# A decoder layer on one core: self-attention with a longer lag between its engines, and another order where cross-attention begins

## The reference, cut to what matters

```
x = layernorm(x + self_attention(x))            # 32 heads of 16, ALiBi bias, causal mask, biases b_qkv and b_out
x = layernorm(x + cross_attention(x, ctx))      # 32 query heads of 128, 8 key/value heads, rotary positions, mask
x = layernorm(x + ffn(x))                       # relu^2 FFN of 1024, plus routed latent path, own layernorm inside
```

## Time and profile before

| | us |
|---|---|
| median of 3 runs | 930.53 (929.92 to 932.32) |
| profiled execution | 930.1 |
| its span, first to last instruction | 928.3 |
| busy in the span: TensorE | 875.9 (94%) |
| VectorE | 679.0 (73%) |
| ScalarE | 487.6 (53%) |
| GpSimd | 497.0 (54%) |
| mean granted TensorE clock | 0.986 of full |
| moved by DMA | 96.65 MB |

### The profile page before, as it was taken

How to read it: one execution, slowest core, us unless ns; L and a number is a source line. 1 busy time by engine, 2 the same in 40 slices (tenths; PEclk the granted TensorE clock), 3 DMA queues, 4 the chain that set the end, 5 groups by cost and what they waited for, 6 DMA issues and landing times.

```text
span 928.3 us, 15683 instructions
## 1 busy us (share of the span) xinstructions
PE 875.9 (94%) x4780; PEld 722.0 (78%) x4780; DVE 679.0 (73%) x2203; ACT 487.6 (53%) x1541; POOL 497.0 (54%) x422
## 2 busy tenths in 40 slices
PE   7998889999997989999999999999999998999996
PEld 6786667777775778888888888888888887787884
DVE  5557678988887677777777777777777778556646
ACT  5327678787786255555555555555555556341320
POOL 4625832242227566666666666666666688564001
PEclk9999899999999989999999999999999999999998
DMA  8678987696566401131311312213113122000000
GB/s 279 246 200 228 243 140 159 160 178 142 126 183 224 162 34 35 35 126 35 128 43 35 125 35 73 88 35 126 35 35 126 41 73 93 18 29 24 24 12 34
DMA packets 68371, 96.65 MB, mean 104 GB/s; under 512 B 7232, under 2 KB 44352, under 8 KB 67264
## 3 DMA queue, kind: packets, MB, share of 16 engines
q1 hardware_dynamic: 68288, 95.65, 36.4%
HBM read 68.33 MB, written 27.26 MB: 103 GB/s over the span
## 4 chain that ended last, share of the span: by engine, by line
PE 64%; DVE 13%; issue 8%; ACT 7%; POOL 5%; DMA 1%; SPq 1%; POOLq 0%; ACTq 0%; DVEq 0%
PE banks L35 55%; PE banks L1107 4%; ACT B_prob L677 3%; DVE B_prob L838 3%; PE banks L1087 3%; PE banks L1108 2%; DVE B_t L902 1%; DVE B_t L903 1%; POOL x L1624 1%; DMA heads_k<-heads_k_d 1%; ACT B_v_out L655 1%; POOL C_t L1212 1%; DVE B_t L898 1%; ACT C_prob L1038 1%; POOL B_wv L171 1%
## 5 line engine op out<-in xcount | busy, mean ns | idle before, releaser
L35 PE MATMUL banks<-C_wo,C_o 128*128 128x512 f32 x768 | 191.2, 398 | 1.9 <-DVE C_o L1199 1.0
L35 PE MATMUL banks<-xT,C_w 128*128 128x512 f32 x768 | 185.6, 390 | 3.1 <-DVE xT L137 1.5
L35 PEld LDWEIGHTS banks<-xT,C_w 128*128 128x128 f32 x768 | 143.9, 188 | 33.9 <-issue 4.2
L35 PEld LDWEIGHTS banks<-C_wo,C_o 128*128 128x128 f32 x768 | 140.2, 189 | 30.4 <-issue 1.9
L1029 ACT ACTIVATE C_q<-C_t 128x512 fp32r<-128x512 f32 x64 | 40.5, 632 | 166.0 <-POOL C_t L1212 166.0
L677 ACT ACTIVATE B_prob<-B_prob,B_top 128x128 f32<-128x128 f32 x256 | 99.4, 392 | 33.4 <-DVE B_top L838 33.2
L1220 POOL TENSOR_TENSOR C_q<-C_t,C_q 128x512 fp32r<-128x512 f32 x64 | 82.9, 1295 | 47.5 <-ACT C_q L1029 47.5
L1038 ACT ACTIVATE C_prob<-C_prob,C_top 128x128 f32<-128x128 f32 x256 | 99.0, 391 | 1.2 <-DVE C_top L1171 1.2
L1212 POOL TENSOR_TENSOR C_t<-C_t,C_t 128x512 f32<-128x512 f32 x64 | 82.7, 1293 | 5.1 <-DVE C_t L1152 4.9
L171 POOL TENSOR_TENSOR C_w<-stage,C_w 128x512 fp32r<-128x512 f32 x32 | 41.8, 1308 | 53.7 <-ACT C_w L166 53.7
L171 POOL TENSOR_TENSOR C_wo<-stage,C_wo 128x512 fp32r<-128x512 f32 x32 | 41.1, 1287 | 54.2 <-ACT C_wo L166 54.2
(11 more groups left out here) (146 smaller groups left out, 1916.4 us busy)
## 6 DMA issues: line engine op xcount, KB each, us to landing
C_kv<-cross_kv_d SPq DMA_DIRECT2D x8, 2048.0 KB, 8.7
cross_kv_d<-B_k_out SPq DMA_DIRECT2D x16, 512.0 KB, 3.3
cross_kv_d<-B_v_out SPq DMA_DIRECT2D x16, 512.0 KB, 4.9
stage<-wq_dram SPq DMA_DIRECT2D x32, 256.0 KB, 2.6
stage<-wo_dram SPq DMA_DIRECT2D x32, 256.0 KB, 2.6
heads_q<-heads_q_d SPq DMA_DIRECT2D x96, 64.0 KB, 3.9
heads_k<-heads_k_d SPq DMA_DIRECT2D x96, 64.0 KB, 4.0
heads_q_d<-cT SPq DMA_DIRECT2D x8, 512.0 KB, 2.6
```

The lines of the kernel that those rows point to most:

```text
L35: mm = eng.matmul(out, stationary[i], moving[j], start=first and n == 0, stop=last and n == len(PASSES) - 1)
```

## The change

Five things are changed, all in order, lag or place; no arithmetic is added or left out.

1. Lags in B: `LT` 2 to 3, `LV` 4 to 6, the whole closing of a batch two steps later (`OT` 11 to 13 and so on); `value_lo` one step after `value_hi` instead of in the same step; `key_lo` and both stores one step later.
2. The output bias `bout` moves to memory of its own (126 KB; there a weight half of cross-attention is written at step 61, which now waits for the eighth addition). So the first oT tile no longer waits for all additions. Each batch's x row is loaded in its step 1 and gets the bias in its step 5.
3. SyncE loads the last four context pieces ahead of the first heads.
4. The `_end` parts are written in another order, with one more transpose, weighing and row addition in them, and query tiles spread between.
5. Cross steps 0 to 2 have orders of their own: `tensor_first` (transposes between the halves of a query tile), `vector_first`, and on ScalarE the exponentials of step 1 behind the pT copy in step 2, and tile 6's high half behind the o copy.

The diff, with little of its unchanged surroundings:

```diff
@@ -305,14 +305,13 @@
                 self.load_piece(eng, self.CONTEXT + (i - self.QK // 2) // 2)
+        for n in range(self.CONTEXT + C, len(self.pieces)):
+            self.load_piece(eng, n)
         heads.wait_stored(eng, self.QK // 2)
...
             ring.load(eng, n, sources[n])
-            if n == 0:
-                for j in range(self.CONTEXT + C, len(self.pieces)):
-                    self.load_piece(eng, j)
         heads.load(eng, 0, 1)
@@ -448,7 +447,7 @@
-    LT, LV = 2, 4
+    LT, LV = 3, 6
     NS = B * NG
@@ -458,7 +457,7 @@
-    OT, CLOSE, ROW, ROOT, NORMAL, TURN, TAKE = 11, (12, 13), 14, 15, 16, 17, 18
+    OT, CLOSE, ROW, ROOT, NORMAL, TURN, TAKE = 13, (14, 15), 16, 17, 18, 19, 20
     NEXT_LOAD = {57: range(5), 62: (5, 6), 64: (7,), 67: (8,)}
@@ -473,7 +472,7 @@
         self.k_out = [pool(f"k_out{i}", (96, 132)[i], [P, 4, 2, S], F32R) for i in range(2)]
-        self.bout = pool("bout", 100, [P, D])
+        self.bout = pool("bout", 126, [P, D])
         self.oT = [pool(f"oT{i}", 100 + 2 * i, [P, C, S], F32R) for i in range(2)]
@@ -533,22 +532,22 @@
                 self.heads.load(eng, later, i)
-            if n < B:
-                eng.dma_start(self.x1[:, n, :], self.dram["x_nat"][:, n, :]).then_inc(self.s_x[n], 16)
+            if n < self.NS and n % NG == 1:
+                eng.dma_start(self.x1[:, n // NG, :], self.dram["x_nat"][:, n // NG, :]).then_inc(self.s_x[n // NG], 16)
             if n == 1:
-                eng.wait_ge(self.before.s_acc, len(self.before.order))
+                eng.wait_ge(self.before.s_vlo, self.before.QK)
                 eng.dma_start(self.bout[:, :], self.dram["bout"]).then_inc(self.s_bout, 16)
...
                 loaded += 1
-            j = self.tile("k", n, 3)
+            j = self.tile("k", n, 4)
             if j is not None:
...
                    .then_inc(self.s_kout[j % 2], 16)
-            j = self.tile("v", n, 1)
+            j = self.tile("v", n, 2)
             if j is not None:
@@ -584,12 +583,18 @@
-        j = self.tile("k", n, 2)
+        j = self.tile("k", n, 3)
         if j is not None:
...
             self.rows.root(eng, b)
+        if n % NG == 5:
+            b = n // NG
+            if b == 0:
+                eng.wait_ge(self.s_bout, 16)
+            eng.wait_ge(self.s_x[b], 16)
+            eng.tensor_tensor(self.x1[:, b, :], self.x1[:, b, :], self.bout[:, :], ALU.add).then_inc(self.s_xadd, 1)
         j = self.tile("k", n, 1)
@@ -597,30 +602,29 @@
         self.gpsimd_pieces(eng, n)
-        b = n - 3
-        if 0 <= b < B:
-            if b == 0:
-                eng.wait_ge(self.s_bout, 16)
-            eng.wait_ge(self.s_x[b], 16)
-            eng.tensor_tensor(self.x1[:, b, :], self.x1[:, b, :], self.bout[:, :], ALU.add).then_inc(self.s_xadd, 1)
         if n in self.NEXT_SPLIT:
+            if self.NEXT_SPLIT[n] == 1:
+                eng.wait_ge(self.s_xadd, B)
             self.cross.piece_lo(eng, self.NEXT_SPLIT[n])
...
+        self.rows.root(eng, B - 2)
         self.key_lo(eng, len(self.FILL) // 2 - 1)
-        for i in range(3, 7):
+        for i in (3, 4):
             self.cross.piece_lo(eng, i)
         self.cross.tile_sum(eng, 0)
+        self.cross.piece_lo(eng, 5)
         self.cross.tile_lo(eng, 0)
-        self.cross.piece_lo(eng, 7)
         self.cross.tile_sum(eng, 1)
+        self.rows.root(eng, B - 1)
         self.cross.tile_lo(eng, 1)
-        self.rows.root(eng, B - 1)
+        self.cross.piece_lo(eng, 6)
         for r in (2, 3):
...
             self.cross.tile_lo(eng, r)
+        self.cross.piece_lo(eng, 7)
@@ -644,8 +648,6 @@
         wait(eng, self.s_y, b)
-        if b == 0:
-            eng.wait_ge(self.s_xadd, B)
         eng.activation(self.oT[0][:, :, :], self.ov[b % 2].rearrange("p (c s) -> p c s", c=C), ACT.Copy).then_inc(self.s_ohi, 1)
@@ -689,16 +691,19 @@
-        self.copy_turned(eng, self.NS - 2)
+        self.copy_turned(eng, self.NS - 3)
         self.key_hi(eng, len(self.FILL) // 2 - 1)
         self.value_hi(eng, len(self.FILL) // 2 - 1)
+        self.copy_turned(eng, self.NS - 2)
+        self.copy_turned(eng, self.NS - 1)
         eng.wait_ge(self.s_klo, len(self.FILL) // 2)
-        for i in range(3, 7):
+        for i in (3, 4):
             self.cross.piece_hi(eng, i)
-        self.copy_turned(eng, self.NS - 1)
         self.rows.hi(eng, B - 2)
+        self.output_hi(eng, B - 1)
+        for i in (5, 6):
+            self.cross.piece_hi(eng, i)
         self.cross.tile_hi(eng, 0)
-        self.output_hi(eng, B - 1)
         self.cross.piece_hi(eng, 7)
@@ -811,19 +816,21 @@
-        self.weigh(eng, (self.NS - self.LV) // 2)
+        self.transpose(eng, self.NS - 3)
+        self.weigh(eng, self.NS // 2 - 3)
         self.transpose(eng, self.NS - 2)
-        self.cross.project(eng, 0)
-        self.cross.project(eng, 1, (0, 1))
+        self.cross.project(eng, 0, (0, 1))
         self.transpose(eng, self.NS - 1)
+        self.weigh(eng, self.NS // 2 - 2)
+        self.cross.project(eng, 0, (2, 3))
         self.turn(eng, B - 2)
-        self.cross.project(eng, 1, (2, 3))
         self.weigh(eng, self.NS // 2 - 1)
-        self.cross.project(eng, 2, (0, 1))
+        self.cross.project(eng, 1)
         self.close(eng, B - 1, range(C))
-        self.cross.project(eng, 2, (2, 3))
-        self.cross.project(eng, 3)
+        self.cross.project(eng, 2)
+        self.cross.project(eng, 3, (0, 1))
         self.turn(eng, B - 1)
+        self.cross.project(eng, 3, (2, 3))
@@ -901,7 +908,7 @@
             eng.tensor_tensor(by_batch(t2[64:128, :]), by_batch(bank[0:64, :]), sin[64:128], ALU.mult).then_inc(self.s_sin, 1)
-        j = self.tile("v", n, 0)
+        j = self.tile("v", n, 1)
         if j is not None:
@@ -912,12 +919,13 @@
         self.norm(eng, self.NS - 1)
+        self.add_row(eng, B - 2)
+        self.value_lo(eng, len(self.FILL) // 2 - 1)
         self.rows.normalise(eng, B - 2)
-        self.value_lo(eng, len(self.FILL) // 2 - 1)
         eng.wait_ge(self.s_klo, len(self.FILL) // 2)
         self.cross.rotate(eng, 0)
+        self.output_lo(eng, B - 1)
         self.rows.lo(eng, B - 2)
-        self.output_lo(eng, B - 1)
         self.cross.rotate(eng, 1)
@@ -1045,13 +1053,23 @@
             eng.activation(self.pT[0][:, :], self.tp[n % 2], ACT.Copy).then_inc(self.s_phi, 1)
-        if n + self.PRE < self.TILES:
+        if n == 2:
+            self.exponentials(eng, 1)
+            self.next_piece_hi(eng, 1)
+        elif n + self.PRE < self.TILES:
             self.tile_hi(eng, n + self.PRE)
...
             eng.activation(self.o[0][:, :], self.ov, ACT.Copy).then_inc(self.s_ohi, 1)
-        self.exponentials(eng, n)
+        if n == 2:
+            self.tile_hi(eng, n + self.PRE)
+        if n != 1:
+            self.exponentials(eng, n)
+            self.next_piece_hi(eng, n)
+    def next_piece_hi(self, eng, n):
         i = self.split(n)
@@ -1135,10 +1153,19 @@
+        if n + self.PRE + 1 < self.TILES:
+            self.project(eng, n + self.PRE + 1)
+    def tensor_first(self, eng, n):
         if n == 0:
             self.project(eng, self.PRE)
-        if n + self.PRE + 1 < self.TILES:
-            self.project(eng, n + self.PRE + 1)
+        self.project(eng, n + self.PRE + 1, range(2))
+        self.transpose(eng, n)
+        self.project(eng, n + self.PRE + 1, range(2, C))
+        self.scores(eng, n)
+        self.values(eng, n)
@@ -1174,29 +1201,51 @@
+    def inverse(self, eng, m):
+        if 0 <= m < self.NS:
+            eng.wait_ge(self.s_exp, m + 1)
+            wait(eng, self.s_norm, m - 1)
+            eng.reciprocal(self.rden[:, m % 2, :], self.total[:, m % 2, :]).then_inc(self.s_rden, 1)
+    def turned_lo(self, eng, m):
+        if 0 <= m < self.NS:
+            eng.wait_ge(self.s_phi, m + 1)
+            eng.tensor_tensor(self.pT[1][:, :], self.tp[m % 2], self.pT[0][:, :].bitcast(F32),
+                              ALU.subtract).then_inc(self.s_plo, 1)
+    def output_lo(self, eng, m):
+        if 0 <= m < self.NS:
+            eng.wait_ge(self.s_ohi, m + 1)
+            eng.tensor_tensor(self.o[1][:, :], self.ov, self.o[0][:, :].bitcast(F32), ALU.subtract).then_inc(self.s_olo, 1)
+    def vector_first(self, eng, n):
+        if n < 2:
+            self.rotate(eng, n + self.PRE)
+        self.turned_lo(eng, n - 2)
+        self.inverse(eng, n - 1)
+        self.minima(eng, n)
+        self.output_lo(eng, n - 2)
+        if n == 2:
+            self.rotate(eng, n + self.PRE)
     def vector(self, eng, n):
-        if n == 1:
+        self.inverse(eng, n - 1)
+        if n + self.PRE < self.TILES:
             self.rotate(eng, n + self.PRE)
-        if self.live(n, 1):
-            eng.wait_ge(self.s_exp, n)
-            wait(eng, self.s_norm, n - 2)
-            eng.reciprocal(self.rden[:, (n - 1) % 2, :], self.total[:, (n - 1) % 2, :]).then_inc(self.s_rden, 1)
-        if n != 1 and n + self.PRE < self.TILES:
```

(21 more changed lines are left out.)

## The result

The changed kernel takes 921.39 us (median of 4 runs, 919.03 to 922.9) where the kernel before took 930.22 beside it: a ratio of 0.990, 95% interval 0.9869 to 0.9932. It is faster, by 8.8 us and not by the 17.3 forecast. The profiled execution took 922.72 us, its span is 920.9.

What follows compares the result with a forecast made beforehand. It took the loop as bound by VectorE's round with a 2.1 us wait, TensorE close behind and full from 337.5 us. Terms 9 + 6.8 + 1.5 = 17.3 off 930.1 gave 912.8, plus 0.4 for the median: 913, range 903 to 926.

Steps and rivals of the forecast that it cites:

- the likeliest case: Whole run: all three gains arrive, 17.3 us in sum, giving 913 us, own range 907 to 919; chance 0.52.
- Part 1: Start of the self-attention loop: spread x loads and bias additions save 9 us, bounds 3 and 11.
- scores of step 8 at 98.6: Start, TensorE: with fewer x loads ahead of batch 1's heads, these scores come at 98.6 instead of 100.97 us.
- rival (b): Start stays DMA-bound, head loads being small and slow; it gains only 3 us, total 919; chance 0.12.
- Part 2: Self-attention loop: VectorE's 2.1 us and TensorE's 0.9 us waits go; batch 25.53 to 24.4, gain 6.8 us, bounds 0 and 10.4.
- A bare VectorE step takes 1.71 us: Loop: VectorE's step without passes, taken as 1.71 us in the eight-step table that closed the round at 24.15 us.
- rival (c): GpSimd's moved bias additions hold up VectorE's divisions, 0.6 to 1.3 us in seven batches; total 917 to 922; chance 0.11.
- Part 3: Last batch and first cross steps to TensorE's second value product: 1.5 us saved of 49.5, bounds -3 and +8.
- The queue in cross step 2: Rotation, sum, copy, exponentials, next rotation and pT half in a row put the second value product 46.2 us after the loop.
- (a): Loop keeps its period, the value half waiting at TensorE's projection; Part 2 gives nothing, total 920; chance 0.13.
- (d): ScalarE becomes the bound in steps 4 and 5, VectorE waiting for oT half and inverse; total 937; chance 0.08.
- (e): Waits only change their names, all three parts near nothing; total 930; chance 0.04.

Runs made afterwards that it cites:

- the middle of the eleven: The eleven kernels with the x loads of the change: VectorE's step 16 from 122.1 to 128.8 us, the middle one at 126.5.
- part 1 alone: Kernel before with only x loads one per batch, bias additions in step 5 and bias load as in the change, lags and orders old: 925.7 us.
- e8_clear_of_divisions: Changed kernel with GpSimd's key half, weight split and bias addition moved to places meant to have no VectorE division: 915.1 us.
- e6: Changed kernel with ScalarE's and VectorE's order of cross steps 0 to 2 as before, TensorE's new order kept: 918.1 us.
- e9: Kernel before with the change's x loads, additions and bias load, plus VectorE's value half one step later; transposes and other lags old: 922.0 us.
- e12_cross_all_before: Changed kernel with the order of the first three cross steps as before on all three engines, the last batch's new order kept: 918.3 us.
- e3: Changed kernel without the eight output-bias additions on GpSimd, so its result lacks that bias: 921.0 us.
- e7: Changed kernel with first value weight pieces split a step earlier and last two output weight pieces loaded behind batch 1's heads: 919.2 us.

## Why the prediction was right, and its terms were not

The direction and the reason for the loop's wait were right, the start is the largest part as forecast (the loop, forecast second, came last), and 921.4 lies inside 903 to 926, but above the likeliest case's own 907 to 919. The sum 17.3 was made of 9 + 6.8 + 1.5; measured were 5.8 + 1.0 + 2.3, and 1.7 lost behind, where I had no term. A gain of half the forecast inside a wide range is in part luck: the loop's term, the best argued, brought a seventh of what it was to bring.

**Part 1, 9 forecast, 5.8 measured (6.8 by the middle of the eleven).** Right: one x load per batch, no wait for the eighth addition, and the cause (6.4 with part 1 alone). Mis-sized: the step "scores of step 8 at 98.6". They came at 100.30: the twelve head loads were issued 1.3 us earlier (from 86.61 on in place of 87.89) and the large transfers ended about as much earlier, but then the small loads moved at some 110 GB/s and not at the 383 by which I had priced the bytes, and landed 0.7 earlier. That is rival (b) in part: its price, 3, was too low, since the other half of the gain (no wait at the first output product and no low clock behind it, 0.68 and 0.90 before and 1.00 after in 116 to 124 us) was real. From the scores of step 8 to step 16 it took 27.2 us where I had 25.0; that batch's divisions took 8.12 us (6.13 before), and the clock was at 0.50 from 102 to 104 again, but what each cost isn't shown. The moved context loads, costed at nothing and at most 2: the first value product begins at 81.72, at 81.57 before and at 81.17 with part 1 alone, so 0.5 at most.

**Part 2, 6.8 forecast, 1.0 measured.** Right: both waits named are gone, the late passes are where I put them, and with nothing in the way the period is 24.4 (24.37 in e8_clear_of_divisions); the 24.4 was my table's 24.15 with a correction. The step that failed is "A bare VectorE step takes 1.71 us", with a division of 0.69 in it, used for all eight. Eight of them take 6.67 us a batch instead of 5.80, because the later steps put the key half and the weight split of GpSimd in front of them. That is rival (c)'s mechanism, near its smaller price (0.5 for 0.6 a batch), with another culprit: I had weighed the rule for the one pass that the change moves, the addition, which meets no division, and not for those that move with a lag or stay while VectorE moves. Four batches are 0.47 us short of the forecast, 1.9 of the missing 5.8. The batch with new value weights is the larger part: I left its extra 1.6 us as it was, and it went from 27.18 to 28.75, 2.7 us short. There two divisions take 1.75 and 1.36 us, the normalisation 1.48 for 0.53, the root stands behind the splits, and the clock falls after a wait of 1.98 us, which alone is 1.2 us by the three executions that kept it. The last batch (25.57, before 25.48) is 1.2 short; its divisions went from 5.85 to 7.41 us.

**Part 3, 1.5 forecast, 2.3 measured.** The queue in cross step 2 came as described: a wait of 2.65 us before the transpose of step 1, the clock at half after it, a second one before the value product, 47.18 us for 48.0 forecast. The 48.0 were 46.2 for the queue and 1.8 for the half clock, and neither was so: in the seven kernels with this order TensorE waited 1.00 to 3.92 us before the value product, and it came 47.16 to 47.19 us after the loop. It waits for the queue, a slow clock before it costs nothing, and the queue is 1.0 us longer than I had it. That the sum came near is luck. What I did not ask is whether the order that causes the queue earns anything: it costs 0.2 to 1.7 us (45.97 without it in e6). Nor is all of the 2.3 shown to be the edits': e9, without them, has 47.53.

**Behind it.** 1.7 us are lost where no instruction changed. In the changed kernel's execution the clock fell around a wait of 1.25 us at 836 us; in e12_cross_all_before, with 1.29 us there, it did not:

```profile
830.00:840.00 10.00, 8.75 (x40) 6.92 (x39) 6.78 (x15) 0.77 (x2) 4.25 (x5) 0.90 0.07 26
840.00:850.00 10.00, 10.00 (x46) 8.32 (x45) 5.20 (x14) 0.77 (x2) 1.53 (x2) 0.93 0.08 29
```
```profile
830.00:840.00 10.00, 8.71 (x43) 7.04 (x42) 6.74 (x16) 0.77 (x2) 3.47 (x4) 1.00 0.08 28
```

At 0.90 and 0.93 over 20 us, 1.0 + 0.7 us of clock are gone, which is the loss. Over the fourteen profiled executions the stretch behind the value product takes either 590.8 to 591.1 us (four, the kernel before and three others) or 592.4 to 592.7 (ten); in three of the ten the third value product comes 9.2 us after the second and not 7.6. The clock accounts for all fourteen: those three have a mean of 0.89 or 0.90 in the 16 us behind the value product, the other seven of the ten 0.91 in 20 us around the wait of 1.25 to 1.29, and the four have 1.00 in both. A forecast can't know on which side a kernel will fall.

**What bounds the kernel.** The prediction read a mean clock of 0.90 over the first and the last stretch as some 10 us at half clock and 5 us of work. At 0.90 a fifth of the 105 us is at half clock, 21 us, and 10 us of work are lost; its bound of 37 us should have been 42. Nothing in the forecast rests on it.

**The rivals.** (a), (d) and (e) did not come: no new wait over 1 us in a steady batch, VectorE waits 0.49 us for oT, ScalarE is busy for 20.62 of 24.85. (b) and (c) came in part. Their prices lead to the same times (917 to 922), so that the time lies there tells neither; by the stretches the start is 3.2 us short, the loop 5.8, the tail 0.8 better and 1.7 lost behind it.

## What to carry to other kernels

When a lag is changed, every pass of the other engines that meets the moved one has to be laid beside it again, not only the pass that the change names: where passes of two engines stretch each other, as here, the phase of a loop is worth part of a microsecond. A set of lags can be a loss alone (27.03 for 25.53) and, beside another, a small gain (24.85 for 25.10), so count the four corners; here one corner, a single lag with part 1, gave all of the time that can be measured. And a new order at a place that was waiting anyway should be set beside the old order, all else as changed, before it is believed.

## What the runs showed of the hardware

The granted clock falls after some waits and not after others of the same size, with the same code: in the batch with new value weights, with 1.97 or 1.98 us of waiting before the turn, the mean was 0.94 in the changed kernel and in e3 (28.8 us) and 1.00 in e6, e7 and e12 (27.5); 24 products behind a wait of 1.25 us in the feed-forward part took 7.35 us in the changed kernel, and 5.73 behind one of 1.29 in e12. So waits of 1.25 to 3.4 us on TensorE cost their length and, at some times, 1.2 to 1.7 us more; where TensorE then waits for a queue of the others, as at the value product of cross step 1, nothing more. Four runs of the changed kernel spread over 3.9 us, and this may be why the medians of kernels whose loops differ by 2 us overlap here; the clock of the unprofiled runs by stretch isn't known.
